# A three-stage transformer chain on one core: attention B in fp16 pieces, with q and k turned by the DMA queue

## The chip, the cores and the metric

The kernel runs on one core of one Trainium2 chip. The time is that of the device in microseconds (us), the median of several executions. The engines are named as in the profile: PE (TensorE, matmuls and transposes), PEld (its weight loads), DVE (VectorE), ACT (ScalarE), POOL (GpSimd) and SP (SyncE, which here only issues DMAs).

## What is computed

Input x has 1024 tokens of 512 numbers. Four layers follow one another, each added to x: attention A, a mixture layer, attention B, and the mixture layer again. The change touches attention B:

```python
w = (qw.astype(jnp.float32) - ZERO) * jnp.repeat(scales, GS, axis=0)   # 4-bit weights, a scale for each 128 rows
q = (h @ w_q)  ; k = (h @ w_k) ; v = (h @ w_v)      # 32 heads of q, 8 of k and v, 128 wide; h = layernorm(x)
q = _apply_rope(q, cos, sin); k = _apply_rope(k, cos, sin)
scores = jnp.einsum('bhqd,bhkd->bhqk', q, k) / math.sqrt(HD)
scores = jnp.where(causal[None, None], scores, jnp.finfo(scores.dtype).min)
attn = jax.nn.softmax(scores.astype(jnp.float32), axis=-1).astype(q.dtype)
ctx = jnp.einsum('bhqk,bhkd->bhqd', attn, v)
x = x + _dequant_matmul(ctx, qw_o, scales_o)
```

In this reference excerpt the three projections stand in one line; each dequantises its own weights.

## The kernel before

Attention B is 64 steps: 8 groups (one k head with its R = 4 q heads, index g) by 8 tiles of 128 tokens (index t). Step u = 8g + t takes the scores of token tile t against the keys of tiles 0 to t, so its softmax rows are n = 128(t+1) long and steps grow with t. The steps of group 0 and the first two of group 1 are written out, then a loop runs over pairs of groups, and the last six steps are written out again. Every engine has its own `step` function, and the order of calls in it is the order on that engine; semaphores tie the engines together.

Each product is made of three matmuls, by the helper `products` (L1408 to L1410): high times high, high times low, low times high. Before the change the pieces of x, of the weights, of q and k, and of the context are fp32r (4 bytes); those of the probabilities and of v are fp16.

What happens in step u, engine by engine:

- PE (`step`, after L1494): keys of head 0 for step u (waits `s_ql`, the pieces of q and k); `project_all(u + 1)`, 24 matmuls for q, k and v of the next step; keys of head 1; half of the output product of step u - 2; keys of head 2; the other half; keys of head 3; `turn_b(u + 1)`, five 128x128 transposes of the rotated q and k from `rc1` (tile `tmp`) into PSUM; `values` of step u - 1, 3t matmuls of 512 columns (24 for t = 0). Then the next step's keys of head 0. Each head's keys end with a mask matmul (L1472).
- DVE: the low parts of heads 2 and 3 of the probabilities of step u - 1 (L1026), the row maxima of the four heads (`maximum`, L1015), the rotation of q and k of step u + 1 from PSUM (L997, L1009, L1011), `turned(u + 1)` (L1032 and L1036: low pieces of q and k), which stands behind the maximum of head 3, and further small steps. In steps t = 4 to 7 it also dequantises the next group's weights (L934).
- ACT: the four exponentials (L665), the high parts of the probabilities (L673), `turned(u + 1)` (L637, L638: high pieces of q and k), behind the high parts of heads 0 and 1. In step t = 6 it rounds the next group's weights ahead of these (L598).
- POOL: adds the two halves of the rotation (L493), and low parts of weights.
- SP: in steps t = 3 to 6 the loads of the next group's weights (12, 12, 4 and 4 DMAs), then for each head a DMA transpose of its probabilities (L447, from `hl` into `hlT`, one of whose two buffers shows up as `fw` in the profile), each waiting for DVE's low part. So the transposes of heads 2 and 3 of step u are issued in the time of step u + 1.

Because `hlT0` lies over the mixture's weights `fw`, those are saved to DRAM and loaded again near the end.

Of the kernel before, what the change touches and what calls it, by code (L numbers as in the profile page):

```python
# [55 lines left out]
PSCALE = 2.0 ** 15  # L56

# [16 lines left out]
def build(nc, x_d, wq_d, bq_d, wk_d, bk_d, wv_d, bv_d, wo_d, bo_d,  # L74
# [6 lines left out]
    with ExitStack() as ctx:  # L81
# [18 lines left out]
        svT = sb("svT", [P, KC, G])  # L100
        sgv = sb("sgv", [P, 3, G])
# [17 lines left out]
        with ExitStack() as mem:  # L119
# [21 lines left out]
            bo = scoped(mem, "bo", [P, D])  # L141
        wo = xT[:, 0:2, :].rearrange("p a (b n) -> p (a b) n", b=2)
# [3 lines left out]
        with ExitStack() as mem:  # L146
            xTh, xTl = (scoped(mem, f"xT{c}", [P, KC, S], F32R) for c in "hl")
            wh, wl = (scoped(mem, f"w{c}", [P, KC, BW], F32R) for c in "hl")
            woh, wol = (scoped(mem, f"wo{c}", [P, R, D], F32R) for c in "hl")
            st = scoped(mem, "st", [P, KC * BW + R * D])  # L150
            scale = scoped(mem, "scale", [P, 2, BW])
            qTh, qTl = (scoped(mem, f"qT{c}", [P, R, P], F32R) for c in "hl")
            kTh, kTl = (scoped(mem, f"kT{c}", [P, S], F32R) for c in "hl")
            vh, vl = (scoped(mem, f"v{c}", [P, T + 2, P], F16) for c in "hl")
            cTh, cTl = (scoped(mem, f"cT{c}", [P, R, P], F32R) for c in "hl")
# [127 lines left out]
        s_rpa = sem("s_rpa")  # L283
        s_vl = sem("s_v_lo")
        s_vb = sem("s_vb")
        s_qkT = sem("s_qkT")
        s_qke = sem("s_qke")
        s_sc = sem("s_sc")
        s_nb = sem("s_nb")
# [1273 lines left out]
```

## Time and profile before

| | us |
|---|---|
| median of 3 runs | 1661.92 |
| lowest and highest | 1657.54, 1664.38 |
| the profiled execution, its own time | 1654.98 |
| its span | 1653.2 |
| PE busy in the span | 1537.8 (93%) |
| DVE busy | 1212.0 (73%) |
| ACT busy | 854.7 (52%) |
| POOL busy | 255.1 (15%) |
| mean granted PE clock, share of full | 0.971 |

Times below are of the profiled execution, counted from the start of its span. Attention B takes the stretch from 631.9 us, the first keys matmul, to about 1585 us. A busy time of PE counts overlapping matmuls, so the distance from one start to the next tells more than a duration.

### The profile page before, as it was taken

What the parts mean: (1) busy time and instruction counts of PE and PEld (TensorE: products, weight loads), DVE (VectorE), ACT (ScalarE), POOL (GpSimd) and SP (SyncE); (2) the same over time, 40 slices, a digit from 0 to 9 for tenths busy, and PEclk for the clock granted to TensorE, in tenths of its full rate; (3) what the DMA queues carried; (4) which work ended last, traced back from release to release, by engine and by line L of the source; (5) the groups of instructions that cost most, each with busy time, mean ns of one, the idle gap of its engine ahead of it and who ended that gap; (6) DMA issues with size and microseconds to landing.
All of it is one profiled execution on the core that took longest, in us unless ns stands there. A gap on an engine that the chain in (4) does not pass through costs nothing.

```text
span 1653.2 us, 25343 instructions
## 1 busy us (share of the span) xinstructions
PE 1537.8 (93%) x7932; PEld 928.9 (56%) x7932; DVE 1212.0 (73%) x2306; ACT 854.7 (52%) x1468; POOL 255.1 (15%) x174
## 2 busy tenths in 40 slices
PE   5689999999999997999999998999999999999979
PEld 3313333323233456777767776776766767767744
DVE  4388888888882586786886886885886877877764
ACT  2106766666677133554564564554564555645531
POOL 2102000000000221232122122132032122212020
PEclk9859999999999997999999999999999999999999
DMA  4992000000001341673763862862863854853631
GB/s 112 141 163 79 1 1 0 0 0 0 0 0 14 98 128 26 143 150 71 164 137 64 183 131 55 184 131 59 177 134 71 177 114 85 174 102 58 144 68 51
DMA packets 369511, 148.32 MB, mean 90 GB/s; under 512 B 323688, under 2 KB 341480, under 8 KB 369136
## 3 DMA queue, kind: packets, MB, share of 16 engines
q1 hardware_dynamic: 369392, 146.87, 43.4%
q8 instruction: 57, 0.93, 0.2%
q14 instruction: 62, 0.51, 0.1%
HBM read 61.33 MB, written 7.90 MB: 42 GB/s over the span
## 4 chain that ended last, share of the span: by engine, by line
PE 69%; DVE 15%; issue 5%; ACT 5%; DMA 4%; SPq 2%; ACTq 0%; POOL 0%; DVEq 0%
PE ps L1408 9%; PE ps L1190 9%; PE ps L1410 8%; PE ps L1409 8%; PE ps L1243 7%; PE ps L1229 6%; DVE hl L1026 4%; PE ps L1370 3%; PE ps L1489 3%; PE ps L1491 3%; PE ps L1490 3%; DVE nmb L1015 3%; DMA hlT<-hl 2%; DVE mx L818 2%; PE ps L1333 2%
## 5 line engine op out<-in xcount | busy, mean ns | idle before, releaser
L818 DVE TENSOR_REDUCE mx<-ps 128x1 f32<-128x512 f32 x512 | 327.7, 686 | 65.4 <-PE ps L1190 63.2
L665 ACT ACTIVATE x<-ps,nmb 128x128 f32<-128x128 f32 (+7 forms) x256 | 188.8, 743 | 287.9 <-DVE nmb L1015 287.9
L579 ACT ACTIVATE proj<-ps 128x1024 f32<-128x1024 f32 x256 | 248.4, 1021 | 124.5 <-PE ps L1229 123.6
L1026 DVE SCALAR_TENSOR_TENSOR hl<-x,rden,hl 128x128 f16<-128x128 f32 (+7 forms) x256 | 225.1, 879 | 33.1 <-ACT hl L673 22.2
L1190 PE MATMUL ps<-ks,qs 96*128 (+1 forms) x512 | 199.4, 413 | 33.2 <-DVE pieces L843 15.1
L673 ACT ACTIVATE hl<-x,rden 128x128 f16<-128x128 f32 (+7 forms) x256 | 184.2, 767 | 53.6 <-DVE rden L1022 52.0
L493 POOL TENSOR_TENSOR tmp<-tmp 128x640 f32<-128x640 f32 x64 | 100.4, 1569 | 701.6 <-DVE tmp L1011 701.6
L1015 DVE TENSOR_REDUCE nmb<-ps 128x1 f32<-128x128 f32 (+7 forms) x256 | 191.7, 749 | 3.5 <-PE ps L1472 3.4
L1408 PE MATMUL ps<-wh,xTh 128*128 128x256 f32 (+1 forms) x512 | 180.6, 353 | 0.0
L1409 PE MATMUL ps<-wl,xTh 128*128 128x256 f32 (+1 forms) x512 | 174.3, 341 | 0.0
L1410 PE MATMUL ps<-wh,xTl 128*128 128x256 f32 (+1 forms) x512 | 173.6, 339 | 0.0
L1408 PE MATMUL ps<-kTh,qTh 128*128 128x512 f32 (+3 forms) x384 | 140.4, 366 | 28.0 <-DVE kTl L1036 13.2
L1190 PEld LDWEIGHTS ps<-ks,qs 96*128 (+1 forms) x512 | 45.0, 97 | 210.6 <-DVE mx L818 140.4
L1229 PE MATMUL ps<-qs,ks 99*128 (+1 forms) x512 | 152.7, 383 | 1.1 <-ACT proj L579 0.8
L1243 PE MATMUL ps<-proj,vcur 128*32 128x512 f32 x1024 | 137.2, 608 | 0.6 <-ACT proj L579 0.6
L1410 PE MATMUL ps<-kTh,qTl 128*128 128x512 f32 (+3 forms) x384 | 132.8, 346 | 0.0
L1409 PE MATMUL ps<-kTl,qTh 128*128 128x512 f32 (+3 forms) x384 | 132.7, 346 | 0.0
L1408 PE MATMUL ps<-woh,cTh 128*128 128x512 f32 x256 | 111.4, 435 | 1.8 <-DVE cTl L1047 1.6
L1408 PEld LDWEIGHTS ps<-kTh,qTh 128*128 128x128 f32 x384 | 72.3, 188 | 64.1 <-ACT x L665 29.1
L1408 PEld LDWEIGHTS ps<-wh,xTh 128*128 128x128 f32 x512 | 99.3, 194 | 8.9 <-issue 0.2
L1410 PEld LDWEIGHTS ps<-wh,xTl 128*128 128x128 f32 x512 | 98.3, 192 | 10.7
L1409 PEld LDWEIGHTS ps<-wl,xTh 128*128 128x128 f32 x512 | 98.9, 193 | 8.0 <-issue 0.2
(177 smaller groups left out, 2498.2 us busy)
## 6 DMA issues: line engine op xcount, KB each, us to landing
st<-in_L_attn_b_qw_q_dram SPq DMA_DIRECT2D x32, 256.0 KB, 3.1
scale<-n_L_attn_b_scales_q_dram SPq DMA_DIRECT2D x32, 256.0 KB, 3.5
st<-in_L_attn_b_qw_o_dram SPq DMA_DIRECT2D x32, 256.0 KB, 3.4
scale<-n_L_attn_b_scales_o_dram SPq DMA_DIRECT2D x32, 256.0 KB, 4.1
qs<-scratch SPq DMA_DIRECT2D x24, 256.0 KB, 8.4
scratch<-pieces SPq DMA_DIRECT2D x5, 768.0 KB, 13.2
xnat<-attn_a_hidden_state_dram SPq DMA_DIRECT2D x8, 256.0 KB, 4.6
x<-attn_a_hidden_state_dram SPq DMA_DIRECT2D x4, 512.0 KB, 18.8
```

The source lines that it names most:

```text
L579: nc.scalar.activation(pbuf[:, e % 4, :].rearrange("p (b n) -> p b n", b=2), ps[:, b:b + 2, :], ACT.Exp, scale=float(HD) ** -0.5).then_inc ...
L665: nc.scalar.activation(pr[:, h, 0:n], flat(2 * (h % 2), n), ACT.Exp, bias=nmb[:, h:h + 1], accum_out=den[:, h:h + 1]).then_inc(s_eb, 1)
L673: nc.scalar.activation(hl[:, h, 0:n], pr[:, h, 0:n], ACT.Copy, scale=rden[:, h:h + 1]).then_inc(s_hi, 1)
L818: nc.vector.tensor_reduce(mx[:, f, k // 2, k % 2:k % 2 + 1], ps[:, bank(k), :], AX.X, ALU.max).then_inc(s_mx, 1)
L1015: nc.vector.tensor_reduce(nmb[:, h:h + 1], flat(2 * (h % 2), n), AX.X, ALU.max, negate=True).then_inc(s_nb, 1)
L1026: nc.vector.scalar_tensor_tensor(hl[:, h, n:2 * n], pr[:, h, 0:n], rden[:, h:h + 1], hl[:, h, 0:n], ALU.mult, ALU.subtract).then_inc(s_lo, 1)
L1190: mm(ps[:, bank, :], qs[0:STACK, ds(g * R + h, 1), f * HALF + qt * P:f * HALF + (qt + 1) * P], ks[0:STACK, ds(g, 1), kh * HALF:(kh + 1) * ...
L1229: ins = mm(ps[:, 4 + 2 * r + j, :], ks[0:STACK + NEG, ds(g, 1), kt * P:(kt + 1) * P], qs[0:STACK + NEG, ds(g * R + 2 * r + j, 1), f * HALF ...
L1243: ins = mm(ps[VW * j:VW * j + VW, 3, :], vcur[:, kt, :], pbuf[:, 2 * (kt % 2) + j // 2, (j % 2) * HALF:(j % 2 + 1) * HALF], start=(kt == 0 ...
L1408: mm(out, lh, rh, start=(start and i == 0), stop=False)
L1409: mm(out, lh, rl, start=False, stop=False)
L1410: ins = mm(out, ll, rh, start=False, stop=(stop and i == len(left) - 1))
```

## The change

All fp32r pieces of attention B become fp16. To fit them into fp16's range, tokens are scaled by `XSCALE`, each group's weight scales are divided by their largest value and multiplied by `WSCALE` (`normalise_scales`, on DVE in the last group of attention A, over rows of 2048, 512, 512 and 2048 scales on 8 partitions), and go to DRAM and back. The largest values come back as `factors`. A group's factor then scales the scores: the exponential takes it as its scale, and every row maximum is multiplied by it in an instruction of its own (L1048 of the new kernel). The other factor goes into the final `add`.

q and k are no longer turned by PE. ACT and DVE split the rotated q and k in token order, from SBUF, into `qkp`, and SP issues two DMA transposes for each step, one of 8 blocks of 128x128 (q) and one of 2 (k). PE waits for both (`s_qkt`) ahead of the keys of head 0. `project_all` gets waits on `s_rope` and `s_vl` that `turn_b` had implied.

`hlT0`, norm statistics and the mixture's small tiles get memory of their own, so that saving and reloading `fw` falls away.

```diff
+XSCALE = 2.0 ** 10
+WSCALE = 2.0 ** 12
+HEADROOM = 2.0 ** 3
...
-            xTh, xTl = (scoped(mem, f"xT{c}", [P, KC, S], F32R) for c in "hl")
-            wh, wl = (scoped(mem, f"w{c}", [P, KC, BW], F32R) for c in "hl")
-            woh, wol = (scoped(mem, f"wo{c}", [P, R, D], F32R) for c in "hl")
+            xTh, xTl = (scoped(mem, f"xT{c}", [P, KC, S], F16) for c in "hl")
+            qT = scoped(mem, "qT", [P, 2, 2 * R, P], F16)
+            kT = scoped(mem, "kT", [P, 2, T, 2, P], F16)
+            qkp = scoped(mem, "qkp", [P, 2 * BH * P], F16)
...
-            sp.dma_start(fw_d, fw[:]).then_inc(s_fws, 16)
...
+            def turned(v, t, par):
+
+                hold(s_ql, v * 2 + 2)
+                if not (isinstance(v, int) and v < 2):
+                    hold(s_sc, (v - 1) * R)
+                sp.dma_start_transpose(qT[:, t % 2], qkp[:, 0:2 * R * P]).then_inc(s_qkt, 16)
+                sp.dma_start_transpose(kT[:, par, t], qkp[:, 2 * R * P:]).then_inc(s_qkt, 16)
...
+                    if h == 0 and not (isinstance(g, int) and g == G - 1 and t == T - 1):
+                        turned(u + 1, after(g, t)[1], par if t < T - 1 else 1 - par)
...
-            def turned(v, t):
-                act.wait_ge(s_qkT, v + 1)
-                nc.scalar.activation(qTh[:].rearrange("p h n -> p (h n)"), ps[:, 6, :], ACT.Copy, scale=SC_B).then_inc(s_qke, 1)
-                nc.scalar.activation(kTh[:, t * P:(t + 1) * P], ps[:, 7, 0:P], ACT.Copy).then_inc(s_qke, 1)
...
+            def turned(v):
+                act.wait_ge(s_rpa, v + 1)
+                if not (isinstance(v, int) and v == 0):
+                    act.wait_ge(s_qkt, v * 32)
+                nc.scalar.activation(qkp[:, 0:R * P], rc1[:, 0:R * P], ACT.Copy,
+                                     scale=HEADROOM / (XSCALE * WSCALE)).then_inc(s_qke, 1)
+                nc.scalar.activation(qkp[:, 2 * R * P:2 * R * P + P], rc1[:, R * P:], ACT.Copy,
+                                     scale=HEADROOM / (XSCALE * WSCALE)).then_inc(s_qke, 1)
...
-                                         accum_out=den[:, h:h + 1]).then_inc(s_eb, 1)
+                                         scale=factor[:, par, 0:1], accum_out=den[:, h:h + 1]).then_inc(s_eb, 1)
...
+            def normalise_scales():
+
+                dve.wait_ge(s_sn, 16 * 4)
+                for i, (r0, n, _, _) in enumerate(SCALES):
+                    rows = slice(r0, r0 + G)
+                    nc.vector.tensor_reduce(top[rows, 0:1], sn[rows, 0:n], AX.X, ALU.max,
+                                            apply_absolute_value=True).then_inc(s_snn, 1)
+                    dve.wait_ge(s_snn, 2 * i + 1)
+                    link(nc.vector.tensor_scalar(top[rows, 0:1], top[rows, 0:1], 1e-30, None, ALU.max))
+                    link(nc.vector.reciprocal(top[rows, 1:2], top[rows, 0:1]))
+                    nc.vector.tensor_scalar(sn[rows, 0:n], sn[rows, 0:n], top[rows, 1:2], WSCALE,
+                                            ALU.mult, ALU.mult).then_inc(s_snn, 1)
...
-            def maximum(u, h, n):
+            def maximum(u, h, n, par):
                 dve.wait_ge(s_sc, u * R + h + 1)
-                nc.vector.tensor_reduce(nmb[:, h:h + 1], flat(2 * (h % 2), n), AX.X, ALU.max, negate=True).then_inc(s_nb, 1)
+                nc.vector.tensor_reduce(nmr[:, h:h + 1], flat(2 * (h % 2), n), AX.X, ALU.max, negate=True).then_inc(s_mxb, 1)
+                dve.wait_ge(s_mxb, u * R + h + 1)
+                nc.vector.tensor_scalar(nmb[:, h:h + 1], nmr[:, h:h + 1], factor[:, par, 0:1], None,
+                                        ALU.mult).then_inc(s_nb, 1)
...
+                nc.vector.scalar_tensor_tensor(qkp[:, R * P:2 * R * P], rc1[:, 0:R * P], HEADROOM / (XSCALE * WSCALE),
+                                               qkp[:, 0:R * P], ALU.mult, ALU.subtract).then_inc(s_ql, 1)
+                nc.vector.scalar_tensor_tensor(qkp[:, 2 * R * P + P:], rc1[:, R * P:], HEADROOM / (XSCALE * WSCALE),
+                                               qkp[:, 2 * R * P:2 * R * P + P], ALU.mult, ALU.subtract).then_inc(s_ql, 1)
...
-            def turn_b(v):
-                pe.wait_ge(s_rpa, v + 1)
-                pe.wait_ge(s_vl, v + 1)
-                for h in range(BH):
-                    dst = ps[:, 6, h * P:(h + 1) * P] if h < R else ps[:, 7, 0:P]
-                    ins = nc.tensor.transpose(dst, rc1[:, h * P:(h + 1) * P], ident[:])
-                ins.then_inc(s_qkT, 1)
...
-                pe.wait_ge(s_ql, u * 2 + 2)
-                keys(g, t, 0)
+                pe.wait_ge(s_qkt, u * 32 + 32)
+                keys(g, t, 0, par)
```

How the order moves shows at three places. On PE, at the end of step t = 1 of group 0, from the last keys matmul to the next step's first; before:

```order
L1472 MATMUL ps<-mask,identb 128x128
L1433 MATMUL ps<-ident,tmp 128x128 [waits s_v_lo,s_rpa]
L1433 MATMUL ps<-ident,tmp 128x128 x4
L1489 MATMUL ps<-fw,vh 128x512 [waits s_turned3,s_turned2,s_xl,s_turned1,s_turned0]
L1490 MATMUL ps<-fw,vl 128x512
L1491 MATMUL ps<-fw,vh 128x512
L1408 MATMUL ps<-kTh,qTh 128x384 [waits s_eb,s_qk_lo]
```

and after:

```order
L1517 MATMUL ps<-mask,identb 128x128
L1534 MATMUL ps<-hlT,vh 128x512 [waits s_turned3,s_turned2,s_xl,s_turned1,s_turned0]
L1535 MATMUL ps<-hlT,vl 128x512
L1536 MATMUL ps<-hlT,vh 128x512
L1457 MATMUL ps<-kT,qT 128x384 [waits s_eb,s_qk_turned]
```

The five transposes are gone, and the wait of the next step's first matmul is on the DMA transposes in place of DVE's low pieces. On DVE, in the same step, from the maximum of head 2 to the low part of head 1 (`hl`); before:

```order
L1015 TENSOR_REDUCE nmb<-ps 128x1 [waits s_sc]
L1026 SCALAR_TENSOR_TENSOR hl<-x,rden,hl 128x256 [waits s_p_hi]
L1015 TENSOR_REDUCE nmb<-ps 128x1 [waits s_sc]
L1032 SCALAR_TENSOR_TENSOR qTl<-ps,qTh 128x512 [waits s_qke]
L1036 TENSOR_TENSOR kTl<-ps,kTh 128x128
L1026 SCALAR_TENSOR_TENSOR hl<-x,rden,hl 128x256 [waits s_p_hi]
```

and after:

```order
L1046 TENSOR_REDUCE nmr<-ps 128x1 [waits s_sc]
L1048 TENSOR_SCALAR nmb<-nmr,factor 128x1 [waits s_max_b]
L1063 SCALAR_TENSOR_TENSOR hl<-x,rden,hl 128x256 [waits s_p_hi]
L1046 TENSOR_REDUCE nmr<-ps 128x1 [waits s_sc]
L1048 TENSOR_SCALAR nmb<-nmr,factor 128x1 [waits s_max_b]
L1069 SCALAR_TENSOR_TENSOR qkp<-tmp,qkp 128x512 [waits s_qke]
L1071 SCALAR_TENSOR_TENSOR qkp<-tmp,qkp 128x128
L1063 SCALAR_TENSOR_TENSOR hl<-x,rden,hl 128x256 [waits s_p_hi]
```

The place of the low pieces of q and k in the row is the same, behind the maximum of head 3; each maximum has got a multiplication behind it. On SP, in steps t = 1 and 2 of group 0; before:

```order
L447 DMA_TRANSPOSE hlT<-hl 128x4x128 [waits s_p_lo,s_tab] x4
L447 DMA_TRANSPOSE fw<-hl 128x6x128 [waits s_tab,s_pvb,s_p_lo]
L447 DMA_TRANSPOSE fw<-hl 128x6x128 [waits s_p_lo,s_tab] x3
```

and after:

```order
L475 DMA_TRANSPOSE hlT<-hl 128x4x128 [waits s_p_lo,s_tab]
L456 DMA_TRANSPOSE qT<-qkp 128x8x128 [waits s_tab,s_sc,s_qk_lo]
L457 DMA_TRANSPOSE kT<-qkp 128x2x128
L475 DMA_TRANSPOSE hlT<-hl 128x4x128 [waits s_p_lo,s_tab] x3
L475 DMA_TRANSPOSE hlT<-hl 128x6x128 [waits s_tab,s_pvb,s_p_lo]
```

The two new transposes stand between those of heads 0 and 1, so six are issued in a step where there were four.

## Rows read from the trace of the kernel before

**Rows 1.** Windows by step: length, busy times (PE, PEld, DVE, ACT, POOL), clock, DMA share, GB/s.

```profile
1191.50:1208.60 17.10, 17.03 (x89) 12.46 (x87) 12.89 (x21) 11.99 (x19) 8.04 (x5) 1.00 0.67 154
1208.60:1227.50 18.90, 18.31 (x90) 12.69 (x91) 17.52 (x26) 10.40 (x18) 3.13 (x2) 1.00 0.61 115
1227.50:1243.10 15.60, 14.59 (x82) 10.54 (x81) 9.74 (x21) 6.00 (x16) 1.57 (x1) 1.00 0.71 113
1281.90:1296.30 14.40, 14.40 (x83) 11.56 (x82) 12.47 (x23) 7.91 (x18) 1.58 (x1) 1.00 0.88 170
631.90:1564.80 932.90, 894.87 (x4758) 674.70 (x4759) 711.67 (x1312) 502.60 (x1066) 196.50 (x123) 0.99 0.59 120
```

**Rows 2.** Timeline of DVE (start, length): the low piece of k in four steps.

```profile
1208.22 0.27 DVE L1036 TENSOR_TENSOR kTl<-ps,kTh 128x128 fp32r<-128x128 f32 x1
...
1225.64 0.28 DVE L1036 TENSOR_TENSOR kTl<-ps,kTh 128x128 fp32r<-128x128 f32 x1
...
1238.59 0.28 DVE L1036 TENSOR_TENSOR kTl<-ps,kTh 128x128 fp32r<-128x128 f32 x1
...
1295.46 0.28 DVE L1036 TENSOR_TENSOR kTl<-ps,kTh 128x128 fp32r<-128x128 f32 x1
```

**Rows 3.** Timeline of all engines at the end of a step t = 4.

```profile
1293.23 0.23 PE L1472 MATMUL ps<-mask,identb 128*128 128x128 bf16 x1
1293.30 0.72 PE L1433 MATMUL ps<-ident,tmp 128*128 128x128 f32 x5
1293.50 0.82 DVE L1015 TENSOR_REDUCE nmb<-ps 128x1 f32<-128x640 f32 x1 [0.32 <-PE ps L1472]
...
1294.55 0.27 ACT L638 ACTIVATE kTh<-ps 128x128 fp32r<-128x128 f32 x1
...
1296.26 0.58 PE L1408 MATMUL ps<-kTh,qTh 128*128 128x512 f32 x1
...
1296.45 0.16 DVE L1019 TENSOR_SCALAR rden<-den 128x2 f32<-128x2 f32 x1
```

**Rows 4.** The tile hl on SP: transposes of 8 blocks, calm, then behind twelve loads.

```profile
DMA to landing us min/median/max: 3.2/3.3/3.4
...
DMA to landing us min/median/max: 4.5/4.9/5.3
```

**Rows 5.** DMA issues in a step t = 0: transposes of 2 blocks, median us to landing.

```profile
fw<-hl SPq DMA_TRANSPOSE x2, 2.3
```

**Rows 6.** Timeline of SP: two transposes back to back, and the first transposes behind loads.

```profile
1286.42 2.65 SPq L447 DMA_TRANSPOSE hlT<-hl  x2
...
1296.10 3.07 SPq L447 DMA_TRANSPOSE fw<-hl  x2
```

**Rows 7.** The chain in a step t = 4, in order of time: start, length until the next.

```profile
1283.74 0.12 PE ps L1409
...
1292.41 0.23 PE ps L1408
...
1293.46 0.56 PE ps L1433 x5
1294.02 0.21 PE ps L1489
```

**Rows 8.** Groups of instructions by form: busy us and mean ns.

```profile
L1026 DVE SCALAR_TENSOR_TENSOR hl<-x,rden,hl 128x512 f16<-128x512 f32 x32 | 23.8, 745 | 0.5
L673 ACT ACTIVATE hl<-x,rden 128x512 f16<-128x512 f32 x32 | 21.4, 716 | 3.1 <-DVE rden L1022 3.1
```

**Rows 9.** Windows: an idle PE, the step t = 2 behind it, and another step t = 2.

```profile
1012.00:1014.70 2.70, 0.00 (x0) 0.00 (x0) 2.52 (x7) 2.51 (x8) 0.00 (x0) 1.00 0.29 49
1014.80:1028.50 13.70, 13.17 (x63) 10.29 (x63) 7.98 (x17) 6.43 (x18) 6.75 (x5) 0.88 0.17 36
...
895.10:907.30 12.20, 11.64 (x63) 9.00 (x63) 9.54 (x21) 7.77 (x21) 6.75 (x5) 1.00 0.24 43
```

**Rows 10.** Timeline of PE in the last group of attention A.

```profile
504.73 0.61 PE L1217 MATMUL ps<-identb,mparts 128*3 128x128 bf16 x8
```

More of the change, by code:

```diff
@@ L285, in build @@
         s_vb = sem("s_vb")
-        s_qkT = sem("s_qkT")
+        s_qkt = sem("s_qk_turned")
         s_qke = sem("s_qke")
@@ L536, in tokens @@
                     nc.scalar.activation(dst, ps[:, turn_bank(phase, t), :].rearrange("p (k n) -> p k n", k=KC),
-                                         ACT.Copy).then_inc(s_xt, 1)
+                                         ACT.Copy, scale=XSCALE if phase == 2 else 1.0).then_inc(s_xt, 1)
             root(0, 0)
@@ L857, in group_a @@
                         maxima(u + 2, f, 0, 6, in_ring)
-                    elif f == 1:
+                    elif f == 0:
+                        normalise_scales()
+                    else:
                         weight(KC - 1)
@@ L1063, in step @@
                     low(u - 1, 2, (one[1] + 1) * P)
-                maximum(u, 0, n)
+                if t == 0:
+                    dve.wait_ge(s_fcr, g + 1)
+                maximum(u, 0, n, par)
                 if exists(*one):
@@ L1069, in step @@
                     rope_sin(t2)
-                maximum(u, 1, n)
+                maximum(u, 1, n, par)
                 invert(u, 0)
@@ L1083, in step @@
                 if exists(*two):
-                    add(u - 2, two[1])
+                    add(u - 2, two[1], par if t >= 2 else 1 - par)
                 if exists(*one):
                     context_low(*one)
+                if t == T - 1 and not last:
+                    group_factor(g + 1, 1 - par)
             def final_statistics(*tiles):
@@ L1137, in tokens @@
                         pe.wait_ge(s_xl, t - 1)
+                    elif phase == 3 and t == 0:
+                        pe.wait_ge(s_rope, G * T * 3)
+                        pe.wait_ge(s_vl, G * T)
                     elif phase == 3 and t in (4, 5):
@@ L1420, in project_all @@
             def project_all(v, g, t):
+                if not (isinstance(v, int) and v == 0):
+                    pe.wait_ge(s_rope, v * 3)
+                    pe.wait_ge(s_vl, v)
                 if t == 0:
@@ L1456, in output_second, with keys @@
                 output(g * T + t, (2, 3))
-            def keys(g, t, h):
+            def keys(g, t, h, par):
                 u = g * T + t
```

211 lines of the change are left out of this document (104 added, 107 removed).

## The prediction, made before the changed kernel was run

> **What bounds the kernel now.** I began with busy time by step. Attention B takes 932.9 us from its first keys matmul to the first of its last step, 63 steps, and PE is busy for 894.9 of them [rows 1]. In the step t = 4 PE has no gap at all. Then DVE, since PE waits at the head of each step for DVE's low piece of k. That piece ends at 1295.74 and the next step's keys start at 1296.26: 0.5 us of slack [rows 2, 3]. At t = 6 it ends at 1208.49 and the next step starts at 1208.60: 0.1, with PE still busy [rows 1, 2]. At t = 7 the slack is 1.6 us (1225.92 to 1227.50), and DVE is busy for 17.5 of 18.9. At t = 0 it is 4.2 (1238.87 to 1243.10), as PE is late with values there. So in most steps two bounds meet: PE's work, and a chain that runs from the last keys matmul through PE's transposes, ACT and DVE to the next step's first matmul. For the four steps without a row I put the slack at 1.5 us together (an estimate: three like t = 6, t = 5 between t = 4 and t = 7), so a group of eight has 8.0 us of it.
>
> **PE's work.** An fp32r matmul of 512 columns takes 0.23 us from start to start, an fp16 one 0.215, and an fp32r one of 256 columns 0.12 [rows 7]. At 256 columns I take half the fp16 price, 0.11. For 128 columns the only 2-byte full row is the mask matmul, 0.07 to the next [rows 3], against 0.11 for each of the five transposes (0.56 by 5, [rows 7]). A step has 12 projection matmuls of 512 and 12 of 256 columns (0.18 + 0.12 = 0.3 us saved), 12 output matmuls (0.18), 12 to 24 keys matmuls (0.3 to 0.5) and the transposes (0.56): 1.3 us, 10.5 a group, 84 in all if PE alone set the pace.
>
> **The new link.** Between DVE's low piece of k and the keys now stand two DMA transposes. q has 8 blocks. The nearest rows are those of hl with 8 blocks, 3.2 to 3.4 us from issue to landing in calm and 4.5 to 5.3 behind twelve loads [rows 4]. k has 2 blocks, 2.3 us [rows 5]. SP takes 2.65 us for two transposes, so k is issued 1.33 behind q [rows 6] and lands at 1.33 + 2.3 = 3.6, behind q. Two semaphores, to SP and to PE, cost some 0.4 together (an estimate; one between PE and DVE is part of the 0.27 from the mask matmul's start to the maximum's [rows 3]). The link is 4.0 us in calm; its bounds are 3.4 and, behind loads, 5.7. It is serial: PE has only `values` between the last keys and this wait, and the maximum of head 3 still stands ahead of the low pieces on DVE, so nothing of it can start sooner. Page "DMA: Bandwidth & Descriptors" of the Trainium skill, section "Rules for kernel authors", says to issue a DMA early and to wait late, since its fixed part then lies beside other work. The row above agrees that this part is there, 2.3 us at two blocks, and this change waits at once.
>
> **Work ahead of the link.** PE's saving ahead of the last keys (all but the transposes) is 0.8 to 1.0 us. Against it, each maximum gets a multiplication of a 128x1 column. The nearest row is 0.16 [rows 3]; with the wait for the reduction that I add, 0.2, and it stands ahead of the exponentials for which PE waits, with ACT queued behind. ACT's q piece goes from 0.6 to 0.72 and DVE's from 0.69 to 0.75 by the rows of the same size from SBUF [rows 8]; the five transposes and ACT's wait for them leave the chain. Net: the low pieces end 0.7 us sooner after the step's start in t = 0 to 5 (-4.2 a group). At t = 6 the chain runs through ACT's rounding of weights and two maxima: +0.4. At t = 7 DVE bounds, and it works off its backlog while PE waits: -1.6 (its 17.5 us and 0.8 of multiplications against 18.9 of step). At t = 3 and 4 SP has twelve loads ahead of head 0's transpose, whose low part at t = 4 is done some 3 us before it is issued at 1296.10 [rows 6], and the transposes land late [rows 4]. I take 1.2 for both steps; the bounds are 0 and 4. Sum: -4.2.
>
> **The sum for a group** is 8 x 4.0 of link, less 8.0 of slack, less 4.2: +19.8 us. Over eight groups, without the last step (0.8), 157.
>
> **PE's clock.** PE idled for over 2.7 us at 1012, and the step behind it ran at a mean clock of 0.88 and took 13.7 us; the same step of another group, at full clock, took 12.2 [rows 9]. So such a fall to the lower of the two levels costs 1.5 us. In the new kernel the way from the last keys to the next is 0.8 + 0.2 (maximum) + 1.0 to 1.4 (low pieces) + 4.0, so 6.0 to 6.4, and `values` covers 0.65t of it. PE idles some 5.5 us at t = 1, 4.7, 5, 3.8, 3.1 at t = 2 to 5, about 5.8 at t = 6, 2 at t = 7, 1 at t = 0. Six of eight are longer than the one in the trace. The slow matmuls behind an idle are keys and projection, and DVE's rotation waits for them: the path. 6 x 1.5 x 8 = 72 us. Below that the cost is 0, above it 3 us a step (144), since the idle is longer here. The page "TensorE: Matmul & The Clock Gate", section "Why this matters for your kernels", warns of just such gaps between bursts of matmuls.
>
> **Attention A.** DVE now reduces and scales 5120 scales in the last group's first half, ahead of `normalise`, for which PE waits at its third key tile, at 504.73 [rows 10]. Reductions at 0.82 us for 640 columns [rows 3] are 6.5 us, scalings between half of that and the same, twelve small links 2: 12 to 15 us, from about 500. PE is held until 512 to 515. The exponentials behind it have slack, and the bound below is 3; I take 8. The saved reload of `fw` was off the path: 0. The other new waits (`s_rope` and `s_vl` ahead of the projection, `s_qkt` ahead of ACT's pieces, `s_sc` on SP) are for things of the step before: 0. The address and casting changes of x, w and the context cost the same: 0.
>
> **The forecast.** 1654.98 + 157 + 72 + 8 = 1892, say 1890 us. The profiled execution was 0.4% below the median of the runs shown, which I leave out.
>
> **Rivals.**
> - The link shows but the clock holds, or its fall lies beside DVE's and ACT's chain: 1655 + 157 + 8 = 1820. For it: at t = 7 and t = 0 DVE sets the pace. Against: the projection is on the path of all others.
> - The queue bounds: six transposes a step, at 1.33 us and more (1.54 at 12 blocks, [rows 6]), are 8 to 10 us of SP, and twelve loads take 6.5 more; if the link is 5.0 in place of 4.0 in all steps, with the clock's fall: 1890 + 63 = 1955.
> - A smaller cost: link 3.4 and the slack larger than I think, no fall: 1655 + 157 - 8 x 8 x 0.6 = 1775 or less, to 1700.
> - Faster: the transposes are hidden. That needs the pieces of q and k to be ready 4 us ahead of PE's need, thus the chain not to be what ends last. Then PE's 84 us come off, less 8: 1655 - 76 = 1580; it decides at a slack of 4 us, which only t = 0 has. The page on TensorE, section "Weight-path perf modes", says that weights of 2 bytes load faster than 4-byte ones; by that rule alone this is the case that wins, and it would change PE's saving, not the link.
> - The change does what it says but PE's fp16 matmuls save nothing (0.23 stays): the forecast grows by under 30 us, within the range.
>
> **Chances.** Forecast 0.50, clock holds 0.25, queue bounds 0.08, smaller cost 0.09, faster 0.06, no change 0.02. The range reaches from 1775 to 1950. A measurement of this kernel tells 0.5% from no change. Faster by more than that 0.06, within it 0.02, slower 0.92.
>
> **What the new profile would show.** PE's first keys matmul of each step waits for the DMA into kT, by 5 us at t = 1 and falling to 2 at t = 7; kT's landing is 2.3 us after its issue; steps at t = 4 of 17 to 19 us; a granted clock of half behind these idles; PE idle for several us before L1217's successor at 504. I am wrong if PE waits at the head of a step for under 2 us, or if something else than PE waits there.

## The result, and the profile after

The changed kernel takes 1912.49 us (median of 4 runs, 1908.26 to 1916.7) against 1660.99 for the kernel before (4 runs beside it): the ratio is 1.1535, with a 95% interval of 1.151 to 1.156. The forecast was 1890, the range 1775 to 1950. The profiled execution has a span of 1910.3 us, 257.1 more than before, and attention B has nearly all of it. It starts at 639.44 in place of 631.9 (+7.5), and its 63 steps take 1184.8 us in place of 932.9 (+251.9). What follows it is 2.3 us shorter.

Three parts of the page of the changed kernel (busy time; clock in the 40 slices; chain), and the group of the keys' first matmul:

```profile
PE 1543.2 (81%) x7612; PEld 705.4 (37%) x7612; DVE 1259.5 (66%) x2583; ACT 873.3 (46%) x1468; POOL 244.9 (13%) x174
...
PEclk9769999999999779888888888888888998988889
...
PE 50%; DVE 22%; DMA 10%; issue 7%; SPq 5%; ACT 4%; DVEq 0%; ACTq 0%; POOL 0%
...
L1457 PE MATMUL ps<-kT,qT 128*128 128x512 f16 (+3 forms) x384 | 137.2, 357 | 286.5 <-DMA kT<-qkp 281.7
```

PE is no longer always busy: it waits 282 us for the transposed k, and in those slices its clock is granted at 0.8 to 0.9. Windows of the changed kernel, with the columns of [rows 1]: steps t = 2, 4, 6, 7 and 0, then all of attention B:

```profile
1276.40:1293.20 16.80, 11.79 (x59) 6.17 (x60) 9.86 (x24) 6.43 (x16) 4.37 (x4) 0.90 0.28 55
1311.40:1331.30 19.90, 15.62 (x76) 7.85 (x76) 12.71 (x27) 8.14 (x16) 1.53 (x1) 0.84 0.70 152
1350.40:1374.40 24.00, 16.99 (x83) 8.58 (x84) 16.16 (x27) 12.67 (x20) 9.32 (x5) 0.88 0.58 127
1374.40:1396.00 21.60, 18.76 (x86) 8.88 (x87) 15.52 (x26) 10.78 (x16) 1.54 (x1) 0.90 0.55 104
1396.00:1411.80 15.80, 14.50 (x76) 7.37 (x76) 8.40 (x24) 4.62 (x16) 1.53 (x1) 0.90 0.76 126
639.40:1824.20 1184.80, 899.93 (x4443) 458.24 (x4444) 750.12 (x1571) 521.91 (x1068) 187.47 (x123) 0.87 0.55 110
```

Against [rows 1] the step t = 4 grew from 14.4 to 19.9 us, t = 6 from 17.1 to 24.0, t = 7 from 18.9 to 21.6, and t = 0 hardly. DVE was busy for 12.5 us of the step t = 4 and is for 12.7 now: no engine has much more work, the steps are longer by waiting. A mean clock of 0.87 over 1184.8 us is some 300 us at the lower of the clock's two levels; the mean was 0.99.

The chain at the end of that step t = 4 (start, length until the next) shows the new link, and its beginning shows the clock:

```profile
1311.42 0.61 PE ps L1457
1312.03 0.43 PE ps L1458
...
1315.87 0.43 PE ps L1457
...
1317.52 0.21 PE ps L1458
...
1324.55 0.89 DVE hl L1063
1325.49 1.71 SPq L475
1327.20 0.05 issue
...
1327.47 1.31 SPq L456
1328.82 2.38 DMA kT<-qkp
1331.20 0.12 issue
1331.32 0.60 PE ps L1457
```

DVE's low piece of k ends at 1327.21. SP issues q at 1327.47 and k at 1328.82, k lands 2.38 later, and the next step's keys start at 1331.32: 4.1 us in place of the 0.5 of [rows 2, 3]. SP's transpose of head 0's probabilities, behind which the two stand in its queue, was over at 1327.20, only just before. In 46 of the 48 steps of groups 1 to 6 it was over before the low piece was made, mostly by 0.15 to 0.5 us and at t = 6 by 2.1, so SP waits for DVE's piece and not the piece for SP. Behind the wait a matmul of 512 columns takes 0.43 us, half the rate of the 0.21 from 1317.52 on. That the wait went before it is what the rows show; what the slow matmuls cost is shown by a run below.

Medians of groups 1 to 6 by step, read from the timelines of both kernels (us; the low piece's end counts from the step's start, the link runs from that end to the next step's keys):

| t | 0 | 1 | 2 | 3 | 4 | 5 | 6 | 7 | sum |
|---|---|---|---|---|---|---|---|---|---|
| low piece of k ends, before | 11.4 | 11.5 | 12.1 | 12.6 | 13.8 | 14.2 | 17.0 | 17.3 | 109.9 |
| the same, after | 11.9 | 10.8 | 13.2 | 14.0 | 15.8 | 15.3 | 20.1 | 17.6 | 118.7 |
| link, before (the old slack) | 4.7 | 0.1 | 0.1 | 0.1 | 0.5 | 1.2 | 0.1 | 1.6 | 8.5 |
| link, after | 3.9 | 3.9 | 3.9 | 4.6 | 3.9 | 3.9 | 3.9 | 4.1 | 31.9 |
| PE idle ahead of the keys, after | 1.2 | 5.8 | 5.1 | 5.4 | 4.0 | 3.6 | 7.0 | 2.9 | 35.0 |

The links cost 23 us a group more than the old slack, and the pieces are ready 9 us later.

### The profile page after: what moved, and what is told of

The parts are those of the page before. It is cut to its first block, busy times and chain, and to the rows that moved or that the text cites. A ratio compares the mean times of both kernels' runs of the same rounds, so it can differ in the third digit from the quotient of the medians.

```text
span 1910.3 us, 25393 instructions
## 1 busy us (share of the span) xinstructions
PE 1543.2 (81%) x7612; PEld 705.4 (37%) x7612; DVE 1259.5 (66%) x2583; ACT 873.3 (46%) x1468; POOL 244.9 (13%) x174
## 4 chain that ended last, share of the span: by engine, by line
PE 50%; DVE 22%; DMA 10%; issue 7%; SPq 5%; ACT 4%; DVEq 0%; ACTq 0%; POOL 0%
DMA kT<-qkp 8%; PE ps L1457 8%; PE ps L1239 8%; PE ps L1458 7%; PE ps L1459 7%; PE ps L1292 6%; DVE nmr L1046 6%; PE ps L1278 5%; SPq L456 4%; PE ps L1419 3%; DVE hl L1063 2%; DVE qkp L1069 2%; DVE mx L847 2%; DVE tmp L1040 2%; PE ps L1382 1%
## 5 line engine op out<-in xcount | busy, mean ns | idle before, releaser
L691 ACT ACTIVATE x<-ps,nmb,factor 128x128 f32<-128x128 f32 (+7 forms) x256 | 210.4, 823 | 586.8 <-DVE nmb L1048 586.7
L1457 PE MATMUL ps<-kT,qT 128*128 128x512 f16 (+3 forms) x384 | 137.2, 357 | 286.5 <-DMA kT<-qkp 281.7
L1046 DVE TENSOR_REDUCE nmr<-ps 128x1 f32<-128x128 f32 (+7 forms) x256 | 192.3, 751 | 101.8 <-PE ps L1517 101.3
L1063 DVE SCALAR_TENSOR_TENSOR hl<-x,rden,hl 128x128 f16<-128x128 f32 (+7 forms) x256 | 212.4, 830 | 25.2 <-ACT hl L699 17.1
L1457 PE MATMUL ps<-wh,xTh 128*128 128x256 f16 (+1 forms) x512 | 205.8, 402 | 0.0
L1458 PE MATMUL ps<-wl,xTh 128*128 128x256 f16 (+1 forms) x512 | 201.6, 394 | 0.0
L1459 PE MATMUL ps<-wh,xTl 128*128 128x256 f16 (+1 forms) x512 | 197.9, 387 | 0.0
L1028 DVE TENSOR_TENSOR tmp<-ps,cosines 128x640 f32<-128x640 f32 x64 | 52.8, 825 | 216.2 <-PE ps L1459 216.2
L1457 PEld LDWEIGHTS ps<-kT,qT 128*128 128x128 f16 x384 | 38.9, 101 | 362.3 <-issue 244.8
L1458 PE MATMUL ps<-kT,qT 128*128 128x512 f16 (+3 forms) x384 | 139.0, 362 | 0.0
L1459 PE MATMUL ps<-kT,qT 128*128 128x512 f16 (+3 forms) x384 | 138.7, 364 | 0.0
L1534 PE MATMUL ps<-hlT,vh 128*128 128x512 f16 x288 | 110.1, 382 | 5.9 <-DMA hlT<-hl 5.7
L1535 PE MATMUL ps<-hlT,vl 128*128 128x512 f16 x288 | 110.0, 382 | 0.0
L1536 PE MATMUL ps<-hlT,vh 128*128 128x512 f16 x288 | 109.9, 382 | 0.0
```

The source lines that it names most:

```text
L691: nc.scalar.activation(pr[:, h, 0:n], flat(2 * (h % 2), n), ACT.Exp, bias=nmb[:, h:h + 1], scale=factor[:, par, 0:1], accum_out=den[:, h:h ...
L1046: nc.vector.tensor_reduce(nmr[:, h:h + 1], flat(2 * (h % 2), n), AX.X, ALU.max, negate=True).then_inc(s_mxb, 1)
L1063: nc.vector.scalar_tensor_tensor(hl[:, h, n:2 * n], pr[:, h, 0:n], rden[:, h:h + 1], hl[:, h, 0:n], ALU.mult, ALU.subtract).then_inc(s_lo, 1)
L1457: mm(out, lh, rh, start=(start and i == 0), stop=False)
L1458: mm(out, lh, rl, start=False, stop=False)
L1459: ins = mm(out, ll, rh, start=False, stop=(stop and i == len(left) - 1))
```

## The experiments

The theory: the transposes cost because they are issued at the last moment and waited for at once, and PE's clock falls behind those waits. The rivals: another part of the change costs (fp16 pieces, factor, new waits), or the queue is overloaded by six transposes a step. All kernels ran beside the kernel before, which took 1653 to 1661 us. e3_fill, e4_longer, e6_ahead and e13_pool_after were executed once.

**The turning alone undone** (e1_pe_turn).

```diff
-                sp.dma_start_transpose(qT[:, t % 2], qkp[:, 0:2 * R * P]).then_inc(s_qkt, 16)
-                sp.dma_start_transpose(kT[:, par, t], qkp[:, 2 * R * P:]).then_inc(s_qkt, 16)
...
+                    ins = nc.tensor.transpose(dst, rc1[:, h * P:(h + 1) * P], ident[:])
```

> The changed kernel with one part of it undone: q and k are turned by five fp32 transposes on TensorE and split from PSUM again, and the first keys matmul waits for DVE's low pieces; the fp16 pieces, the normalised scales and the multiplication behind every maximum stay. Theory A (the DMA turning, with the clock's fall behind its waits, is the whole loss): the chain at a step's head is the old one. Against the kernel before the fp16 matmuls save up to 84 us less the transposes' 36 (these stay), so up to 48, the multiplications give back 0.2 x 2 a step (25) and attention A's last group 8: 1661 - 48 + 25 + 8 = 1645, range 1610 to 1665, and no time at the lower clock to speak of. Theory B (something else of the change costs, the fp16 pieces, the scaling or the new waits): 1700 or more. Theory C: DVE and ACT pace the steps, fp16 saves nothing: 1670 to 1700.

Measured: 1670.15 us, ratio 1.0079 (1.0057 to 1.0102). So the turning in the queue costs 242 of the 251 us, and the rest of the change gains nothing: it is 0.8% slower than the kernel before. Theory A's number was too low by 25 us and its range ended at 1665; the result lies at the lower end of theory C. Windows (t = 1, t = 4, all of B), and DVE's timeline at that t = 4:

```profile
1137.72:1148.59 10.87, 9.57 (x62) 5.67 (x60) 7.12 (x21) 5.38 (x17) 1.54 (x1) 1.00 0.11 22
1172.20:1188.06 15.86, 13.64 (x82) 7.08 (x82) 12.72 (x27) 7.99 (x18) 1.53 (x1) 1.00 0.80 156
639.67:1581.48 941.81, 850.65 (x4758) 448.16 (x4759) 735.51 (x1571) 519.32 (x1066) 185.38 (x123) 0.98 0.57 117
...
1174.17 0.95 DVE L951 SCALAR_TENSOR_TENSOR st<-st,scale 128x768 f32<-128x768 int32 x1
1177.01 0.96 DVE L951 SCALAR_TENSOR_TENSOR st<-st,scale 128x768 f32<-128x768 int32 x1 [1.89 <-DMA scale<-sv_n]
```

At t = 1 the step takes 10.9 us in place of 11.6, just PE's saving (0.74 without the transposes). PE is busy for 851 us in place of 895 [rows 1]. But at t = 4 DVE, at the head of its step, waits 1.9 us for the next group's loads, which have less time to arrive in shorter steps, and PE waits behind it: 15.9 in place of 14.4. This is the longest of the six such steps; their median is 15.3.

**The factor left out of that kernel** (e8_pe_turn_no_factor): no multiplication at L1048, and the exponential's scale is a constant.

> The kernel with q and k turned on TensorE in fp16 pieces, with one part left out: the group's factor on the scores, that is the multiplication behind each maximum and the factor as the exponential's scale (which is a constant 1 here), so the scores are not scaled. Theory A (the factor's 0.25 us on each maximum and 0.08 us on each exponential are what eats the fp16 matmuls' saving): faster than with the factor by 0.25 x 2 to 0.33 x 4 a step, 64 steps: 32 to 85 us, so 1585 to 1638. Theory B (the saving is lost because DVE now waits for the weights' loads at t = 4 and PE for the transposed probabilities at t = 0): at most 15 us faster, 1655 or more.

Measured: 1649.8 us, ratio 0.9944 (0.9921 to 0.9966), 20 us less than with the factor, between the two theories. B takes 923.7 us. The factor costs 20, most of it at t = 0 (18.0 us at the median with it, 15.6 without) and t = 6 (17.8 and 16.6). Without it B is still only 9 us below the old 932.9, where the matmuls alone could save 48; the rest is lost elsewhere.

**PE kept busy in the changed kernel's waits** (e3_fill).

```diff
+                    for _ in range(FILL[t]):
+                        mm(ps[:, 6, :], xTh[:, 0, 0:P], xTh[:, 0, 0:512], start=True, stop=True)
```

> The changed kernel with idle matmuls (128x128 by 512 columns, fp16, into a PSUM bank that nobody reads) behind the values of each step of groups 1 to 6: 0, 22, 18, 20, 14, 12, 27 and 9 of them at t = 0 to 7, which fill all but some 1 us of PE's wait for the DMA. They compute nothing. Theory A (the fall of PE's clock behind its waits costs on the path): the clock stays at the upper level in these groups, the 5.8 us a step at the lower level that the changed kernel's middle groups show become nearly none, and a step shortens by 1.5 to 2.5 us: 6 x 8 x 2 = 96, so 1815, range 1790 to 1845. Theory B (the slow matmuls lie beside the chain on DVE and ACT): within 15 us of 1912.

Measured: 1856.64 us. The window of groups 1 to 6 in the changed kernel:

```profile
791.48:1699.73 908.25, 692.83 (x3432) 352.39 (x3433) 581.57 (x1207) 401.13 (x817) 147.69 (x96) 0.88 0.57 115
```

and with the idle matmuls:

```profile
793.08:1642.26 849.18, 780.46 (x4164) 393.53 (x4165) 578.67 (x1207) 401.15 (x817) 148.43 (x96) 0.99 0.61 124
```

The clock rises from 0.88 to 0.99 and 59.1 us go, by more work on PE: theory A, at a smaller size than 96, and 12 us above the end of its range. That is 9.8 us a group, 79 for eight groups (an estimate, as groups 0 and 7 have no idle matmuls). By the clock column some 200 us less were spent at the lower level; if PE had set the pace in all of them, 100 would have come back, so four tenths of it lay beside other engines' work. With the clock up B is still 22.0 us a group above the old kernel (849.2 against 717.1 for six).

**A longer link** (e4_longer).

```diff
+                sp.dma_start_transpose(spare[:], qkp[:, 0:2 * R * P]).then_inc(s_qkt, 16)
```

> The changed kernel with a third transpose in each step, of q into a tile that nobody reads, issued ahead of the two. It makes the link longer by one issue on SP, 1.3 us. Theory A (the link is serial, nothing covers it): 63 x 1.3 = 82 us more, 1995, range 1980 to 2010. Theory B (part of it lies beside other work): under 30 us more. Theory C (the queue bounds: the transposes delay those of the probabilities and of the loads): over 130 us more.

Measured: 2024.64 us, +112. The end of a step t = 4 in its chain:

```profile
1389.32 1.23 SPq L457
1390.59 1.34 SPq L458
1391.97 2.39 DMA kT<-qkp
1394.36 0.12 issue
1394.48 0.61 PE ps L1459
```

The link's median grew from 3.9 to 5.25 us, and 63 times the difference is 85; over groups 1 to 6 it is 65 of 91 us. The other 26 show as pieces of k that are ready later, by 4.2 us a group, and the clock fell from 0.88 to 0.83, which fits them (some 120 us more at the lower level; at 59 for 200, as in the last run, that is 35, a little too much). The link is serial, with no cover, as theory A has it; but 2024.64 lies 15 above A's range, whose number left the clock's part out, and below theory C's 130 us.

**The pieces made earlier in the step** (e2_early): `turned` on ACT ahead of `high(0)`, on DVE ahead of `maximum(u, 2)`, on SP ahead of head 0.

> The changed kernel with q and k split earlier in each step: ACT ahead of the high parts of heads 0 and 1, DVE ahead of the maximum of head 2, and on SP the two transposes ahead of that of head 0. Same instructions, other order. Theory A (a serial link from the low piece of k to the keys): the low piece of k ends sooner by 1 to 2 us at t = 0 to 3, 3 at t = 4, 5 and 7, and 7 at t = 6, where four roundings of weights stood ahead of it; some 23 us a group less 4 for maxima that come later, so 1912 - 8 x 19 = 1760, range 1680 to 1800. Theory B (SP's queue or the DMA engines bound, not the time at which the pieces are ready): 1880 or more. If all of the link is hidden, PE sets the pace and the time is under 1650.

Measured: 1791.87 us, ratio 1.0824 (1.0791 to 1.0857), so 121 us less: theory A, near the upper end of its range. The low pieces of a group end 22.8 us sooner, as forecast (23), but 8 of these come back as longer ways from there to the keys or as other waits. At t = 6 PE now finds k turned, and the step takes 17.0 us; at t = 2 it still waits 3.8 us. At t = 1 the low piece ends 9.8 us after the step's start and the link adds 4.0, where the whole step took 10.9 in e1_pe_turn: too short for projection, rotation, splitting and transposes one behind the other.

**Two steps ahead** (e6_ahead, and e7_ahead_late with the splitting later in the step).

```diff
-                    project_all(u + 1, *after(g, t))
+                    project_all(u + 2, g2, t2)
```

> The changed kernel with q, k and v projected, rotated, split and turned two steps ahead of their use in place of one: same instructions, at the same places within a step, but for the step after next; v gets a third slot that alternates between groups, and the first two loads, dequantisations and the roundings of a group's weights come one step sooner. Theory A (the link costs because it is waited for at once): the transposes have a whole step to land, PE no longer waits for them, the clock does not fall, and a group is near the 119 us of the old kernel or some us below, B some 900 to 950 us in place of 1185; 1600 to 1680 us. Theory B (the transposes' load on SP and on the DMA engines costs by itself): PE then waits for the transposed probabilities in place of q and k, and the time is over 1750.

> As the kernel with q and k two steps ahead, and the splitting moved back within its step, since nothing waits for it any more: on ACT between the exponentials of heads 2 and 3, on DVE behind the low part of head 1, on SP behind the transpose of head 1. Theory A: the exponentials of head 2 and the probabilities' pieces come 1 us sooner, so it is 0 to 30 us faster than the one before it: 1580 to 1660. Theory B (DVE's total work bounds at t = 4 to 7, the order within a step is all the same): equal within 5 us.

Measured: 1717.03 and 1713.84 us (ratio of the second 1.0318, 1.0291 to 1.0345). The same transposes cost 200 us less when they have a step to land: the queue's load as such isn't what costs most. But both miss theory A's range, and the order within the step is worth little: 3 us, as theory B of the second has it. In the second, windows at t = 1, t = 3 and t = 0, and what waited in groups 1 to 6 (us, times, longest):

```profile
1167.38:1177.12 9.74, 8.83 (x57) 5.07 (x55) 5.98 (x18) 4.16 (x13) 1.54 (x1) 1.00 0.07 15
1188.41:1208.00 19.59, 14.18 (x63) 6.42 (x61) 12.48 (x28) 7.71 (x18) 1.53 (x1) 0.83 0.83 146
1146.97:1167.38 20.41, 15.85 (x78) 7.44 (x76) 11.07 (x30) 6.40 (x17) 1.53 (x1) 0.83 0.67 127
...
PE ps L1470 <- ACT x L698: 64.8, 47, 5.4
...
DVE st L973 <- DMA scale<-sv_n: 40.6, 24, 3.7
PE ps L1547 <- DMA hlT<-hl: 27.9, 8, 4.9
```

t = 1 takes 9.7 us against 11.6 before the change; the windows at t = 3 and t = 0 are among the longest of their kind, with medians of 17.9 and 20.1 us against 12.8 and 16.0. What is lost is lost at t = 3 and 4, where DVE waits for the loads and ACT and PE behind it, and at t = 0, where the transposes of heads 2 and 3 come late; the clock falls there.

**The scales normalised behind the division** (e9_ahead_scales_later).

```diff
-                    elif f == 0:
-                        normalise_scales()
...
+                    if last and f == 0:
+                        normalise_scales()
```

> As the late-splitting kernel that works two steps ahead, and the normalisation of the scales moved behind the division of the third last half group of attention A, where DVE idled for 12 us in the kernel before. Theory A: the 7 us gap on PE at 507 is gone and attention B starts 7 to 8 us sooner: 7 to 8 us faster than without the move. Theory B (the weights that DVE copies behind it are late instead): no gain, within 2 us.

Measured: 1705.12 us, 8.7 less (ratio 1.0269, 1.0246 to 1.0292), as theory A has it; in the profiled executions B starts at 633.2 in place of 644.7, 11.5 sooner, more than the gap explains. In this stretch PE is idle for 0.5 us at most. PE there in the changed kernel, with the gap:

```profile
503.58 1.06 PE L1292 MATMUL ps<-proj,vcur 128*32 128x512 f32 x8
511.78 1.01 PE L1266 MATMUL ps<-identb,mparts 128*3 128x128 bf16 x8 [7.14 <-DVE pieces L872]
```

**Loads and transposes spread out, then loads in pairs** (e10_spread, e11_paired).

```diff
-                        sp.dma_start(stq[:, c, c0:c0 + w].bitcast(I32),
-                                     w_d[c * P:(c + 1) * P, ds(g * w, w)]).then_inc(s_wl[c], 16)
+                        sp.dma_start(stq[:, c:c + 2, c0:c0 + w].bitcast(I32),
+                                     w_d[c * P:(c + 2) * P, ds(g * w, w)].rearrange("(c p) n -> p c n", p=P)).then_inc(s_wl[c], 16)
```

> The late-splitting kernel two steps ahead, scales moved, with what its profile showed as waits mended: the loads of a group's first two chunks of weights stand at t = 2 and 3 without waiting for each other (four buffers for scales in place of two) and DVE dequantises them at the end of steps 3 and 4 in place of the head, where it waited for the loads with PE behind it; on SP the transposes of q and k stand behind that of head 3, with two buffers for their pieces. Theory A (what is left over the old kernel are those waits, not the transposes as such): t = 3 from 16 to 19 us down to 12, t = 4 from 16 to 18 down to 14, t = 0 from 20 down to 17; some 10 us a group, 80 in all: 1625, range 1605 to 1650, which is faster than the kernel before. Theory B (six transposes a step load the DMA engines so that the waits only move): 1660 or more.

> The kernel of the last run, with the loads of a group's weights in pairs: one DMA for two chunks, so 6 in place of 12 at t = 2 and 3, and 2 in place of 4 at t = 5 and 6. In the last run PE waited 2.8 to 5.1 us for the transposed probabilities at t = 3 and 4, which SP issued behind 12 loads of 0.54 us each. Theory A (the time that SP takes to issue the loads sets these waits): they shrink by the 3.2 us of six issues, and the falls of the clock behind them go: 5 to 8 us a group, 1689 - 8 x 6 = 1640, range 1625 to 1655, below the kernel before by 0.3 to 2%. Theory B (the bytes on the DMA engines set them, not the issue): the same bytes in fewer, larger DMAs, 1680 or more.

Measured: 1688.77 us (ratio 1.0173, 1.0147 to 1.0199), then 1659.34 (1.0012, 0.9994 to 1.003). The first missed theory A's range and came out in theory B's: mending the first waits made new ones. In e10_spread no dequantisation waits for long, but PE waits for the probabilities, which SP issues behind twelve loads; and that wait, in groups 1 to 6, is first:

```profile
PE ps L1554 <- DMA hlT<-hl: 58.9, 18, 5.1
```

and with the loads in pairs (e11_paired):

```profile
PE ps L1554 <- DMA hlT<-hl: 45.3, 18, 3.8
```

The same bytes in half the DMAs gave 29 us: the issue on SP counted, as theory A has it, though not all of these waits went, and its range was missed by 4 us. Groups 1 to 6 of the profiled executions got 21.3 us shorter, 13.6 of them in the wait shown.

**The same mending with TensorE's transposes** (e12_pe_turn_paired).

> The kernel in fp16 pieces with q and k turned on TensorE, with the same mending: the scales normalised later, paired loads at t = 3 and 4 into four buffers of scales, and the dequantisations of the first four chunks at the end of steps 4 and 5 in place of the head. Theory A (of its 1670 us, 7 are the scales, and at t = 4 and 5 PE waits for DVE which waits for loads): t = 4 from 15.3 to 13.5, t = 5 from 16.7 to 15, 7 for the scales and some 1 at t = 0: 1670 - 7 - 8 x 4 = 1630, range 1610 to 1645, 1 to 3% below the kernel before. Theory B (DVE's work as such bounds these steps): 1655 to 1665. Against the version with the DMA's transposes two steps ahead it tells whether turning on TensorE or in the queue is better once neither is waited for.

Measured: 1643.96 us, ratio 0.9914 (0.989 to 0.9937): 0.9% below the kernel before, the only whole version that beats it, and 15 us below the best with the DMA's transposes (e11_paired). It just meets the upper end of theory A. Its step t = 4, which took 15.3 us at the median in e1_pe_turn:

```profile
1156.41:1169.54 13.13, 13.13 (x82) 7.33 (x83) 11.25 (x25) 8.19 (x18) 1.54 (x1) 1.00 1.05 203
```

PE has no gap there, and the step is 1.2 us below the old one [rows 1]. But t = 6 grew to 19.5 us, from 17.1 in the kernel before and 17.8 in e1_pe_turn, which takes more than that back.

**POOL kept off the low piece of k** (e13_pool_after).

```diff
+                    pool.wait_ge(s_ql, (g * T + t + 1) * 2 + 2)
                     low_parts(g + 1)
```

> The changed kernel with one wait more: in steps t = 6 POOL starts the low parts of the next group's weights only when DVE's low piece of k is made. In the changed kernel that piece, 128x128 from two SBUF sources, takes 1.72 us at t = 6 in place of 0.28, while POOL works. Theory A (the two share something that only one can hold, as the page SBUF - State Buffer of the Trainium skill, section SBUF: two separate sides, says of a DVE instruction with two SBUF inputs and a GpSimd instruction that reads SBUF): the piece takes 0.28 and ends 1.4 to 1.6 us sooner, so the step t = 6 falls from 24.0 to 22.5; the step behind it gives 0 to 3 us back, since PE then waits for the weights' low parts. In all between 1898 and 1925. Theory B (the piece is slow for another reason, as its place behind the longest maximum): it stays at 1.7.

Measured: 1922.64 us. The low piece at t = 6 in the timeline of the changed kernel, with POOL beside it:

```profile
1365.79 4.58 POOL L525 TENSOR_TENSOR wl<-st,wh 128x768 f16<-128x768 f32 x2
...
1368.79 1.73 DVE L1071 SCALAR_TENSOR_TENSOR qkp<-tmp,qkp 128x128 f16<-128x128 f32 x1
```

and in this one:

```profile
1375.53 0.28 DVE L1072 SCALAR_TENSOR_TENSOR qkp<-tmp,qkp 128x128 f16<-128x128 f32 x1
```

Theory A: 0.28 us in all 64 steps. The step t = 6 falls from 24.0 to 22.5 or 23.4 us, and t = 7 gives it back (25 in place of 21.7): PE waits there for the weights' low parts, 1.5 us, and spends some 9 us at the lower clock in most of these steps in place of 4.6. So the delay is real, and this cure isn't one.

## Why the prediction was right, step by step

The direction, the mechanism and the order of the terms held; the forecast was 1.2% low. Between the profiled executions the time grew by 257.1 us, where 237 was forecast. Of the 20 missing, the link, the slack and the work ahead of the link have 17, the clock 6, attention A -0.5, and what follows attention B -2.3, where the saved reload had been put at 0. Between the medians the time grew by 251.5; the forecast started from the profiled execution, 6 us below the median of the kernel before.

- **The link**, 4.0 us calm, with k landing 2.3 behind its issue: 3.9 and 2.38. A group's eight links take 31.9 us; 32.0 was written. e4_longer shows that it is serial. The Trainium skill's page "VectorE: DVE Perf Modes", section "The three transpose paths", gives 1309 ns for a 128x128 block by DMA against 390 by TensorE. The trace agrees with the order, 2.38 us from issue to landing for two blocks against 0.56 for five transposes on PE [rows 7]; no run here times one block alone, and what the consumer waits for is 3.9.
- **The slack**, 8.0 a group: 8.5. The four steps without a row had 0.1, 0.1, 0.1 and 1.2, 1.5 in all, as estimated; t = 0 had 4.7 in place of 4.2.
- **Work ahead of the link**, -4.2 a group with +1.2 for late transposes in it: in e3_fill, where the clock is up, the pieces end 4.2 us sooner over t = 0 to 5, as written, 1.8 sooner at t = 7 (1.6 written), and 1.5 later at t = 6 (0.4 written). The +1.2 for t = 3 and 4 is 2.1: in e3_fill those two links are 5.4 and 4.5. These three terms together are 20.9 us a group by the medians and 22.0 by the means, in which the slower steps of some groups count, in place of 19.8.
- **The clock**, 72: 79 by e3_fill. A step has 4.6 us at the lower level on average (222 us in 48 steps), and four tenths of what that costs PE is hidden. The rival "the clock holds" is refuted. That the size came out so near is in part luck: 72 was six falls a group at 1.5 us, read from one pair of steps, and in the changed kernel all eight steps of a group have 2.5 us or more at the lower level and give back 1.2 us each. Nor does an idle of this length bring a fall each time. In the kernel before, an idle of 2.9 us has the full clock behind it:

```profile
1253.60:1256.50 2.90, 0.00 (x0) 0.00 (x0) 2.74 (x7) 2.49 (x8) 0.00 (x0) 1.00 0.32 51
1256.70:1260.00 3.30, 3.30 (x22) 2.92 (x23) 0.95 (x2) 1.53 (x3) 0.82 (x1) 1.00 0.38 46
```

- **Attention A**, 8: B starts 7.5 us later, and PE's gap is 7.14.
- **The idles** were forecast at 5.5, 4.7, 5, 3.8, 3.1, 5.8, 2 and 1 for t = 1 to 7 and 0, and are 5.8, 5.1, 5.4, 4.0, 3.6, 7.0, 2.9 and 1.2: half a microsecond short nearly everywhere, and 1.2 at t = 6.
- **Mis-sized**: the step t = 6. "+0.4" for the low piece, measured 3.1 (17.0 to 20.1). About 1.5 of it is the low piece itself beside POOL. I had taken its duration to be that of the old piece, which read PSUM and one SBUF tile; from two SBUF tiles it isn't the same instruction. The rest goes when the clock is up (18.5 in e3_fill, less that 1.5, is the old 17.0). Over seven groups the 1.5 is 10 us of the 20 missed. t = 4 came out at 19.6 us, above the 17 to 19 that I gave.
- **The queue bounds** (1955): not in the changed kernel, whose link is 3.9 us in nearly all steps, but SP's queue does show as a wait as soon as the link is hidden (e10_spread, e11_paired). The condition for the **faster** rival, pieces ready 4 us ahead, was made true in e6_ahead, and 1580 was far off: I had costed nothing for loads and probabilities that must also come sooner in shorter steps.
- **fp16 saves nothing**: at t = 1 to 3 the saving is there as counted (0.7 a step). Over all it is gone (e1_pe_turn), by 20 us for the factor, by waits for loads at t = 4 and 5, and by falls of the clock at t = 0. The weight loads did get shorter, 458 us of PEld in place of 675 in B; what that alone is worth no run shows.

Two steps of the kernels with TensorE's transposes stayed longer than the sums say. At t = 0 e1_pe_turn takes 18.0 us at the median against 16.0, and its six such steps go with the clock: 15.5 and 16.1 us with no time at the lower level, 17.5 and 18.4 with 3.4 us of it, 19.3 and 19.4 with 6.8. In the kernel before, one of the six has such a fall (18.1). Why the clock falls there more often stays open. At t = 6 of e12_pe_turn_paired DVE has four dequantisations ahead of the maximum of head 0:

```profile
1186.56 3.02 DVE L952 SCALAR_TENSOR_TENSOR st<-st,scale 128x768 f32<-128x768 int32 x4
```

where e1_pe_turn has two:

```profile
1208.05 1.28 DVE L951 SCALAR_TENSOR_TENSOR st<-st,scale 128x512 f32<-128x512 int32 x2
```

That is 1.74 us more, and the step is 1.74 longer (19.53 against 17.79). Two of the four are those that the edit moved to the end of step t = 5.

## What to carry to other kernels

A DMA transpose takes no time of PE, ACT or DVE, but between producer and consumer it was here 2.4 us of landing, for two blocks, and 1.3 for each transpose issued ahead of it. Put it at least a whole stage ahead of its use, and then look at what else shares its queue; here TensorE's transposes were still 15 us faster in the end (e12_pe_turn_paired against e11_paired). Before replacing a short chain on compute engines, look at the slack at its end (0.1 us in four of eight steps here): where there is none, every new microsecond is paid once a step, and paid again in the clock if it leaves TensorE idle. A gain of 0.7 us a step on the bounding engine was kept only where the loads and the next engine could follow.

## What the runs showed of the hardware that I had not expected

- A DVE instruction with two SBUF sources is held up while POOL works on SBUF: 1.72 us for a 128x128 piece in place of 0.28. In e13_pool_after, when POOL's low parts fall on other DVE work, two dequantisations of 512 columns take 2.80 in place of 1.28. Reductions from PSUM at the same time aren't slower (1.08 at 1366.73). The page "SBUF — State Buffer" of the Trainium skill, section "SBUF: two separate sides", says so: the pair of ports that the two share is locked for a whole instruction, with DVE instructions that have two SBUF inputs among those that take it. The trace agrees with it. In e13_pool_after L1057, which has one small tile as its source, was slow beside POOL too (1.60 in place of 0.17), and no run here tells why. The kernel before shows the same delay one instruction later, on a low part of the probabilities (1.15 us by itself), when the pieces of q and k, read from PSUM, were already made:

```profile
1208.42 2.70 DVE L1026 SCALAR_TENSOR_TENSOR hl<-x,rden,hl 128x896 f16<-128x896 f32 x1
```

- An exponential that takes its scale from a tile is slower than one with a constant, by the same amount at any length. Groups by form (busy us, mean ns), the changed kernel:

```profile
L691 ACT ACTIVATE x<-ps,nmb,factor 128x1024 f32<-128x1024 f32 x32 | 38.4, 1199 | 75.2 <-DVE nmb L1048 75.2
...
L691 ACT ACTIVATE x<-ps,nmb,factor 128x128 f32<-128x128 f32 x32 | 14.3, 449 | 60.1 <-DVE nmb L1048 60.1
```

and the kernel before:

```profile
L665 ACT ACTIVATE x<-ps,nmb 128x1024 f32<-128x1024 f32 x32 | 35.5, 1115 | 39.1 <-DVE nmb L1015 39.1
...
L665 ACT ACTIVATE x<-ps,nmb 128x128 f32<-128x128 f32 x32 | 11.6, 371 | 26.7 <-DVE nmb L1015 26.7
```

1199 against 1115 ns, and 449 against 371: 0.08 us each, 256 times. In e8_pe_turn_no_factor, where the scale is a constant again, they are 1113 and 371.
